# Attention weighing x itself, with the joint value and output weights applied after the scaling, and a changed start

## What is computed

```python
q = jnp.einsum('bim,mhd->bhid', x, wq)
k = jnp.einsum('bim,mhd->bhid', x, wk)
v = jnp.einsum('bim,mhd->bhid', x, wv)
q = rope(q); k = rope(k)
s = jnp.einsum('bhid,bhjd->bhij', q, k) / 128
s = s - 1e30 * (i < j)
p = jax.nn.softmax(s, axis=-1)
o = jnp.einsum('bhij,bhjd->bhid', p, v)
y = jnp.einsum('bhid,hdm->bim', o, wo)
x = layernorm(x + y)
```

## Time and profile before

| | |
|---|---|
| median of 3 runs | 1671.52 us (1671.47 to 1673.33) |
| profiled execution | 1672.75 us, its span 1670.7 us |
| TensorE busy | 1625.1 us, 97% |
| GpSimd busy | 1413.7 us, 85% |
| VectorE, ScalarE busy | 1244.0 and 1214.0 us |
| granted TensorE clock | 0.995 of full speed on average |

### The profile page before, as it was taken

One profiled execution on the slowest core, in us unless ns is written; L12 is line 12 of the kernel. 1 busy time (PEld: TensorE's weight loads), 2 busy tenths in 40 slices (PEclk: granted clock), 3 DMA queues, 4 the chain that ended last, 5 costly groups with the idle time before them and its releaser, 6 DMA issues. The chain is left out here.

```text
span 1670.7 us, 29885 instructions
## 1 busy us (share of the span) xinstructions
PE 1625.1 (97%) x10452; PEld 1471.7 (88%) x10452; DVE 1244.0 (74%) x2899; ACT 1214.0 (73%) x2427; POOL 1413.7 (85%) x797
## 2 busy tenths in 40 slices
PE   4999999999999999999999999999999997999997
PEld 4899999999999999999999999999999986999997
DVE  5787778777877777778777877787777777677775
ACT  3877777777777777777777777777777764665664
POOL 4799989998999899998999899989998975777884
PEclk8999999999999999999999999999999999999999
DMA  5222232223222322232223222322232323123212
GB/s 151 77 76 75 77 99 71 74 75 98 74 75 74 100 73 75 74 99 76 77 77 102 77 77 77 102 77 76 77 89 76 89 77 102 45 67 96 68 33 58
DMA packets 69763, 134.10 MB, mean 80 GB/s; under 512 B 19312, under 2 KB 38000, under 8 KB 69616
## 3 DMA queue, kind: packets, MB, share of 16 engines
q1 hardware_dynamic: 67856, 130.10, 28.9%
q10 hardware_dynamic: 1760, 2.10, 0.4%
HBM read 56.36 MB, written 8.70 MB: 39 GB/s over the span
## 5 line engine op out<-in xcount | busy, mean ns | idle before, releaser
L506 ACT ACTIVATE probs<-ps_slot,neg_max 128x640 f32<-128x640 f32 (+7 forms) x512 | 381.1, 746 | 154.2 <-DVE neg_max L649 154.2
L649 DVE CUSTOM_DVE_ANT_0 ps_slot<-ps_slot,causal 128x640 f32<-128x640 f32 (+7 forms) x512 | 383.0, 769 | 132.7 <-PE ps_slot L57 132.4
L904 PE MATMUL ps_turn<-ident,probs 128*128 128x128 f32 x2048 | 279.2, 274 | 2.3 <-DVE pt_high L676 1.2
L55 PE MATMUL ps_slot<-k,q 128*128 128x512 f32 (+4 forms) x768 | 274.9, 358 | 6.5 <-DVE v L694 5.1
L57 PE MATMUL ps_slot<-k,q 128*128 128x512 f32 (+4 forms) x768 | 264.9, 345 | 0.0
L56 PE MATMUL ps_slot<-k,q 128*128 128x512 f32 (+4 forms) x768 | 263.1, 343 | 0.0
L904 PEld LDWEIGHTS ps_turn<-ident,probs 128*128 128x128 f32 x2048 | 232.8, 140 | 21.8 <-issue 2.1
L676 DVE TENSOR_TENSOR pt_split<-ps_turn,pt_split 128x512 fp32r<-128x512 f32 x256 | 175.3, 685 | 93.4 <-ACT pt_split L551 93.4
L439 POOL TENSOR_TENSOR q<-rot_q,q 128x1024 fp32r<-128x1024 f32 x63 | 152.2, 2416 | 52.6 <-ACT q L534 52.6
L423 POOL TENSOR_TENSOR swapped_k<-swapped_k,rope 128x1024 f32<-128x1024 f32 x63 | 152.4, 2420 | 42.6 <-DMA swapped_k<-unrot_k 42.5
L417 POOL TENSOR_TENSOR rot_k<-unrot_k,rope 128x1024 f32<-128x1024 f32 x64 | 154.7, 2417 | 16.4 <-ACT unrot_k L516 13.8
(11 more groups left out here) (198 smaller groups left out, 4426.1 us busy)
## 6 DMA issues: line engine op xcount, KB each, us to landing
swapped_k<-unrot_k SPq DMA_DIRECT2D x128, 256.0 KB, 3.6
swapped_q<-unrot_q SPq DMA_DIRECT2D x128, 256.0 KB, 3.6
inv_b<-inv_rows SPq DMA_DIRECT2D x64, 512.0 KB, 4.7
y_t<-y_sum SPq DMA_DIRECT2D x8, 512.0 KB, 5.4
x_raw<-y_t SPq DMA_DIRECT2D x8, 512.0 KB, 4.1
unrot_q<-in_L_attn_x SPq DMA_DIRECT2D x8, 512.0 KB, 5.4
row_b<-r_rows SPq DMA_DIRECT2D x16, 256.0 KB, 3.6
x_raw<-x_cols SPq DMA_DIRECT2D x7, 512.0 KB, 5.3
```

The lines of the kernel that those rows point to most:

```text
L55: pe.matmul(out, stat_hi, mov_hi, start=start, stop=False, skip_group_check=True)
L506: act.activation(probs_tile(t), score_tile(name, head, i), ACT.Exp, scale=-1.0, bias=neg_max[:, head.par, t:t + 1], accum_out=sums[:, head ...
L649: dve.tensor_tensor_reduce(tile, tile, causal[:, T - WIDTH[t]:T], -1.0, UNSEEN, ALU.add, ALU.min, neg_max[:, head.par, t:t + 1]).then_inc( ...
L904: last = pe.transpose(bank[:, at:at + P], probs_tile(t)[:, j * P:(j + 1) * P], ident[:, :])
```

## The change

The probabilities now weigh the tokens x themselves (`x_split`, high and low part, loaded as rows once a batch and split by ScalarE and VectorE). `scale_y` divides as before, and the scaled result of a head is split (`split_y_hi` on ScalarE in two halves, `split_y_lo` on GpSimd in the middle of its step) and multiplied by the head's joint matrix (`project_out`, 6 matmuls of 512 columns, three steps after the head's own). The product is added to `y_sum` by VectorE, straight from the score slot. The values projection, its splits and GpSimd's addition are gone. `project_out` of the last two heads, the last split and the last two additions stand behind the last step.

At the start: ScalarE's first activation is an exponential, so that its function table is loaded at once; the six weight transfers are issued at other places; TensorE does 40 transposes of the identity first; the joint weights are split in step 0 and not before it, and so are the weights of heads 2 to 7 (which lie in `y_head` and `y_sum` now) and the first batch's tokens; VectorE does the first head's sine for q too. `se_t` and `w1_s` take the place of weights of q and k.

```diff
-SLOT_FILLS = {"v": (0, 1), "s32": (1, 1), ...
+SLOT_FILLS = {"out": (0, 3), "s32": (1, 1), ...
@@ GpSimd @@
+            def split_y_lo(head):
+                pool.wait_ge(y_hi, head.made() * 2)
+                pool.tensor_tensor(y_split[:, 1, :], y_head[:, :], f32(y_split[:, 0, :]), ALU.subtract).then_inc(y_lo, 1)
...
                 rotate_add(1, after)
+                split_y_lo(head.step(-2))
                 mul_sin(0, after)
...
-                if not is_step(head, heads):
-                    add_y(before)
@@ ScalarE @@
+            def split_y_hi(head, half):
+                act.wait_ge(y_scaled[half], head.made())
+                if head.step(-1).live():
+                    act.wait_ge(filled["out"], head.step(-1).made())
+                act.activation(y_split[:, 0, half_cols(half)], y_head[:, half_cols(half)], ACT.Copy).then_inc(y_hi, 1)
...
+            act.wait_ge(consts, 1)
+            act.activation(inv[:, 0, :], kept.minus_half[:, :], ACT.Exp)
...
-                if before.live():
-                    split_v_hi(before)
...
+                split_y_hi(head.step(-2), 0)
                 exp("s4", head)
                 turn("3", before)
                 turn_shared(before, head)
...
                 exp("s7", head)
...
+                    if loads_tokens(head, half):
+                        split_tokens_hi(head.batch() + 1, half)
+                split_y_hi(head.step(-2), 1)
+                if is_step(head, 0):
+                    act.wait_ge(wvo_made, 1)
+                    act.activation(wvo_part(0), both_y, ACT.Copy).then_inc(wvo_hi, 1)
                 exp("s6", head)
+                if is_step(head, 0):
+                    split_rest_hi("k", WK_HI, 1.0)
+                    split_rest_hi("q", WQ_HI, 1.0 / P)
+                    for half in range(2):
+                        split_tokens_hi(0, half)
                 split_hi(1, after)
...
             steps(act, step, 16)
+            for half in (1, 0):
+                split_y_hi(Head(0, heads - 1, heads), half)
@@ VectorE @@
+            def add_y(head):
+                dve.wait_ge(filled["out"], head.made())
...
+                    dve.tensor_tensor(y_sum[:, :], slot("out", head), y_sum[:, :], ALU.add).then_inc(y_added, 1)
...
             def scale_y(g, head):
...
-                    dve.wait_ge(y_added, head.step(-1).made())
+                    dve.wait_ge(y_lo, head.step(-1).made())
...
-                split_v_lo(head)
+                if not is_step(head, heads):
+                    add_y(head.step(-2))
                 rowmax("s32", head, 1)
...
             steps(dve, step, 16)
+            add_y(Head(0, heads - 2, heads))
+            final = Head(0, heads - 1, heads)
+            dve.wait_ge(y_hi, final.made() * 2)
+            dve.tensor_tensor(y_split[:, 1, :], y_head[:, :], f32(y_split[:, 0, :]), ALU.subtract).then_inc(y_lo, 1)
+            add_y(final)
@@ TensorE @@
+            def project_out(head):
+                pe.wait_ge(y_lo, head.made())
+                for half in range(2):
+                    cols = half_cols(half)
+                    last = matmul_split(pe, slot("out", head)[:, cols], kept.wvo[:, 0, head.no, :], kept.wvo[:, 1, head.no, :],
+                                        y_split[:, 0, cols], y_split[:, 1, cols], True, True)
+                last.then_inc(filled["out"], 1)
...
-                    v_j = v[head.at // 2 % 2][:, :, j_first + j, head.par, :]
+                    x_j = x_split[head.batch() % 2][:, :, j_first + j, :]
...
                 free_slot(exped[5], before)
-                if not is_step(head, 0):
-                    project_v(before)
+                project_out(head.step(-3))
...
+            for i in range(40):
+                pe.transpose(both_turn[:, i % 8 * P:(i % 8 + 1) * P], ident[:, :], ident[:, :])
...
             steps(pe, step, 16)
+            pe.wait_ge(se_lo, 1)
+            project_out(Head(0, heads - 2, heads))
+            pe.wait_ge(z_lo, 1)
+            project_out(Head(0, heads - 1, heads))
```

204 lines of the change are left out of this document (95 added, 109 removed).

## The result

The changed kernel takes **1688.74 us** (median of 4 runs, 1687.91 to 1689.88) beside 1671.49 for the kernel before on the same chip: a ratio of 1.0101, 95% interval 1.0089 to 1.0112, 17.25 us slower. Forecast were 7.6 us more, 1679.1, with a range up to 1688. The direction was right, the size was not: the loss is over twice as large, just outside the range. In the experiments the kernel before, run beside them, took 1673 to 1674 us; they are compared by their ratio to it.

The account below looks back on a forecast made before the run. TensorE, busy 97% of the span, was taken as the bound. Steps -3.0, start -2.2 and hand-over +12.8 gave +7.6 us on a median of 1671.5, so 1679.1 us, range 1669 to 1688.

Parts of the forecast that it names:

- Steps, TensorE's own work: Steps 3 to 62: six 512-column matmuls replace twelve of 256, gaining 0.05 us a head, 3.0 us in all.
- 0.7 us of slack is left: no cost: Steady steps: GpSimd's added 2.4 us split makes q ready at 729.6, TensorE wants it at 730.29; nothing lost.
- splitting the tokens ... those steps are not longer. Nothing: Steady steps: two more VectorE splits a batch, 2.15 us each as they wait for GpSimd, cost nothing.
- rival 2: Steady steps: GpSimd becomes the bound; q 0.3 us late costs 18 us over 60 steps, about 1697 us; chance 0.10.
- k is done 3.8 us earlier, so the first scores come at 23.2: Start: earlier first projection and less work before the scores bring head 0's first scores 8.2 us earlier.
- rival 1: Start: step 0 hides the moved work, so the 8.2 us gain stays; 1666 us, last block before 40; chance 0.10.
- Half clock behind it: Start: TensorE idles over 3 us twice in step 0's chain, then runs at half clock, costing 2.0 us.
- the prediction's step 2: Start: step 2 has no product yet, which gives 1.5 us.
- (a): Hand-over: steps 63 and 64 hold products, VectorE's additions stand ahead of row maxima; 1.2 us each, 2.4.
- (b): Hand-over: head 63's first scaling waits for ScalarE's late copy and GpSimd's split; 1394.5 instead of 1388.45.
- (c, d): Hand-over: second scaling ends at 1398.0; two additions, split and product follow, second part starts at 1403.7 to 1404.9.
- (e): Second part's start: its first six matmuls run at half clock, up to 1.2 us.

Follow-up runs that it names:

- e4: Changed kernel with the loads of the other heads' weights and the tokens held until the first head's swapped q has landed; ratio 1.0079 to the kernel before.
- e12: Changed kernel with rearranged start, GpSimd's split first, ScalarE's copies paired, k's copy at the step's end, shorter hand-over; 1669.56 us, ratio 0.9974 to the kernel before.
- e2: Changed kernel with ScalarE's two high copies of the scaled result next to each other, ahead of tile 4's exponential; ratio 1.0088 to the kernel before.
- e6: Changed kernel with the joint weights' high copy and low split back ahead of head 0's scores; ratio 1.0087 to the kernel before.
- e7: Changed kernel with paired high copies and a shorter hand-over, products of heads 62 and 63 accumulated together and added once; ratio 1.0061 to the kernel before.
- e11: Changed kernel without the 40 transposes of the identity ahead of its first projection; ratio 1.0093 to the kernel before.

## Why the prediction was right and wrong

- **Steps, TensorE's own work: right in the total, in part by luck.** 0.06 a step against 0.05, 3.6 us against 3.0. The replaced matmuls themselves gave 0.03 (1.51 to 1.48); the other 0.03, in blocks behind them, was not forecast. Followers are spaced by 0.119 us at 256 columns and by 0.232 at 512, so the fixed cost per matmul is 2 x 0.119 - 0.232 = 0.006 us, near the 8 ns read from the earlier trace rows. By the figure of the Trainium skill (TensorE: Matmul & The Clock Gate, on the spacing of back-to-back matmuls) six matmuls would be worth an estimated 15 ns a step; measured are 31 in the replaced matmuls and 60 in the step.
- **Steps, GpSimd: the step "0.7 us of slack is left: no cost" failed.** Its arithmetic was right (the chain's length and q's time). It asked only when TensorE wants q. VectorE's cosine of the next q waits for the same split and is due before that: 0.64 us ahead of the scores is in time, 0.20 is not. ScalarE's high copy of q waits for an earlier link of the same chain, and when a transfer is late it holds up the exponentials behind it. A plain step had no room left for the 0.45 us by which a disturbed one is late. Then "splitting the tokens ... those steps are not longer. Nothing" failed: I had read the 2.15 us of VectorE's split and noted that it waits for GpSimd, but not that GpSimd pays 0.44 us too. In the kernel before, with q split 2.1 us ahead, slack swallowed that in 13 steps (GpSimd's sine of q takes up to 2.87 us there, and the period stays 21.12), and a late transfer with it. This is rival 2 with 0.10, in a mild form: its mechanism, in 34 steps of 60, 0.08 to 0.8 us each. It cost 7.1 us, the largest error.
- **Start: "k is done 3.8 us earlier, so the first scores come at 23.2" failed at one link.** k was done 3.7 earlier, its swap landed only 1.4 earlier, and q's swap kept VectorE waiting for 0.9 more. I had moved the swap against unchanged transfer times, although the change puts the weights' loads right behind it and the tokens' load after it. With the loads held back (e4) the forecast's numbers appear: 23.44 for 23.2, 44.61 for 44.3 to 45.2. The long chain in step 0 was sized well, 21.0 us measured between those two points and 21.1 to 22 forecast, and so was rival 1's condition, a last block before 40: the changed kernel is far from it, and e12, which meets it, wins the start.
- **Half clock behind it:** 2.0 forecast. From the last block to the next step's scores the changed kernel takes 8.22 us where the kernel before takes 6.74, so 1.5; over 44 to 56 us the granted clock is 0.72 where it was 1.00. Windows of the changed kernel, then of the kernel before (columns as in the earlier trace rows):

```profile
44.00:56.00 12.00, 9.82 (x46) 8.42 (x47) 6.92 (x16) 6.48 (x16) 3.54 (x3) 0.72 0.00 0
```

```profile
44.00:56.00 12.00, 10.82 (x73) 9.74 (x71) 8.33 (x19) 10.70 (x23) 6.63 (x3) 1.00 0.11 22
```

- **The stretch without a product** (the prediction's step 2, between the scores of steps 1 and 2) takes 20.64 instead of 21.12, so it gained 0.48 and not 1.5: TensorE had less work there, but waited for the others. Together with the missed 2.7 at the last block this makes +0.98 for the start, 3.2 above the forecast.
- **Hand-over: right, in each link.** (a) step 62 took 21.18 against 20.05, +1.1, and up to ScalarE's copy of the normed rows another 1.1 was lost (1394.67 and 1387.98, 2.25 later counted from step 62), forecast 1.2 each. (b) First scaling of head 63, counted from step 62's scores: 51.56 against 45.68, +5.9, forecast +6.05. (c, d) second part's start +12.46, forecast +11.4 to +12.6 (the terms of (d) add up to 5.4 to 6.6, so these bounds are 0.3 too high); the product took 2.9 us at a granted clock of 0.50, forecast up to 2.6. (e) its first matmuls run at 0.63 us instead of 0.39, but the second part as a whole measured 0.3 less than before, where it scatters by 3.2, so this term can't be told. Total +12.2 for +12.8.

## What to carry to other kernels

When an instruction is put into a chain that has slack, list every engine that waits for the chain's end or for a link of it, not only the bottleneck engine, and take the earliest due time; and keep in mind what the slack was already paying for. A transfer that starts earlier is only worth as much as what now runs beside it allows. A gap on the critical engine's supplier, here GpSimd's wait for a transfer, is the place for added work, provided the engines that read its next result are not held up in their own order.

## What was not expected of the hardware

- A split on VectorE with two SBUF inputs that meets GpSimd costs both: VectorE 2.28 instead of 0.69 us, and GpSimd's next instruction 2.84 instead of 2.39. With 32 columns instead of 512 VectorE still waits, GpSimd does not pay. The eight normalising instructions, with one SBUF input each, took 4.25 instead of 2.13 us beside a GpSimd instruction. The Trainium skill (SBUF — State Buffer, on its two sides) describes a lock of a port pair held for a whole instruction, by which the later one waits; the trace agrees for both.
- In the changed kernel five of the swaps of k (steps 9, 11, 30, 32 and 54) land 0.7 to 1.3 us later than the others. In other kernels such steps stand near the same places: 12, 31, 32, 51 and 54 in e2, 10 to 12, 31, 32 and 53 in e6, 10 to 12, 33 and 54 in e7, but 37, 38, 40, 60 and 61 in e11. Their cause stays open; no run was made on it.
